# Query and key projections as pairs of 64-row products, maxima turned by VectorE, scores 12 groups behind

## The reference

```python
x = layernorm(x + attn(x, w_qkv, w_proj))            # 16 heads of 16, rotary turn of q and k
x = layernorm(x + xattn(x, ctx, Wq, bq, ..., Wo, bo)) # 16 heads of 16, keys and values from ctx
x = layernorm(x + ffn(x, ...))                        # two layers of local attention and MLP
```

## Time and profile before

| | us |
|---|---|
| median of 3 runs (2247.1 to 2249.8) | 2249.5 |
| span of the profiled execution | 2234.3 |
| TensorE busy in it | 2109.7 |
| VectorE busy | 1661.7 |
| ScalarE busy | 1501.9 |
| GpSimd busy | 1327.5 |
| 16-head part: first maximum to last `pv` | 43.0 to 983.2 |

### The profile page before, as it was taken

One profiled execution on the slowest core, in us unless ns is written; L12 is line 12 of the kernel. 1 busy time (PEld: TensorE's weight loads), 2 busy tenths in 40 slices (PEclk: granted clock), 3 DMA queues, 4 the chain that ended last, 5 costly groups with the idle time before them and its releaser, 6 DMA issues.

```text
span 2234.3 us, 44819 instructions
## 1 busy us (share of the span) xinstructions
PE 2109.7 (94%) x13992; PEld 1475.9 (66%) x13992; DVE 1661.7 (74%) x3987; ACT 1501.9 (67%) x3418; POOL 1327.5 (59%) x1376
## 2 busy tenths in 40 slices
PE   3899999999999999977999999899989999998998
PEld 2544444444444444346888888788878888887887
DVE  4777888777888888747888888656388888886675
ACT  2287777777888888855777777554367777775443
POOL 0344555533334444477888877454378887875775
PEclk7699999999999999999999999999999999999999
DMA  7667677665756666434545455300055554552111
GB/s 154 109 125 147 140 146 137 144 143 124 154 136 155 159 160 137 140 101 105 131 109 115 103 115 110 93 26 6 1 138 116 111 113 107 108 114 62 58 62 43
DMA packets 201337, 248.92 MB, mean 111 GB/s; under 512 B 26584, under 2 KB 119512, under 8 KB 201112
## 3 DMA queue, kind: packets, MB, share of 16 engines
q1 hardware_dynamic: 198552, 237.68, 47.7%
q0 software_dynamic: 2560, 8.39, 1.1%
HBM read 97.47 MB, written 63.44 MB: 72 GB/s over the span
## 4 chain that ended last, share of the span: by engine, by line
PE 77%; DMA 5%; POOL 5%; SPq 4%; ACT 3%; DVE 3%; issue 2%; POOLq 0%; ACTq 0%; DVEq 0%
PE PS L485 14%; PE PS L487 12%; PE PS L486 12%; PE PS L606 9%; PE PS L590 8%; PE PS L573 5%; PE PS L699 5%; PE PS L675 5%; PE PS L684 4%; DMA KS<-hs 3%; PE PS L659 2%; SPq L1496 2%; SPq L1464 1%; ACT PT L827 1%; DMA hs<-HL 1%
## 5 line engine op out<-in xcount | busy, mean ns | idle before, releaser
L1003 DVE TENSOR_REDUCE MX<-PS 128x1 f32<-128x512 f32 x1024 | 642.5, 682 | 167.1 <-PE PS L573 156.9
L827 ACT ACTIVATE PT<-PS 128x512 f32<-128x512 f32 x1024 | 546.2, 599 | 129.5 <-PE PS L590 127.6
L573 PE MATMUL PS<-KS,QS 48*128 48x512 f32 x1024 | 357.0, 454 | 43.7 <-DMA KS<-hs 33.5
L590 PE MATMUL PS<-QS,KS 50*128 50x512 f32 x1024 | 385.5, 456 | 6.4 <-ACT PT L827 6.0
L590 PEld LDWEIGHTS PS<-QS,KS 50*128 50x128 f32 x1024 | 164.9, 187 | 270.5 <-issue 212.3
L1369 POOL TENSOR_TENSOR PB<-PB,RC 128x512 f32<-128x512 f32 (+1 forms) x256 | 250.6, 999 | 48.6 <-DVE RC L1123 48.6
L606 PE MATMUL PS<-PT,VP 128*17 128x512 f32 x2048 | 273.6, 606 | 2.9 <-ACT OT L834 2.9
L890 ACT ACTIVATE PB<-PB,NMf 128x256 f32<-128x256 f32 (+1 forms) x512 | 242.6, 478 | 8.6 <-DVE NMf L1114 8.5
L573 PEld LDWEIGHTS PS<-KS,QS 48*128 48x128 f32 x1024 | 171.5, 192 | 108.0 <-issue 59.3
L1349 POOL TENSOR_TENSOR RI<-RI,mhalf 128x8 f32<-128x8 f32 x128 | 214.1, 1672 | 10.7
L1114 DVE CUSTOM_DVE_ANT_0 PB<-PS,mk 128x256 f32<-128x256 f32 (+1 forms) x512 | 175.7, 385 | 54.4 <-PE PS L675 54.2
(11 more groups left out here) (182 smaller groups left out, 5054.4 us busy)
## 6 DMA issues: line engine op xcount, KB each, us to landing
qT<-QN SPq DMA_DIRECT2D x384, 128.0 KB, 2.4
hs<-HL SPq DMA_DIRECT2D x64, 512.0 KB, 3.8
kT<-kT SPq DMA_DIRECT2D x256, 128.0 KB, 2.5
QS<-hs SPq DMA_DIRECT2D x192, 128.0 KB, 5.9
KS<-hs SPq DMA_DIRECT2D x192, 128.0 KB, 8.0
od<-OT SPq DMA_DIRECT2D x64, 256.0 KB, 5.9
OC<-od SPq DMA_DIRECT2D x32, 256.0 KB
cst<-rs SPq DMA_DIRECT2D x32, 256.0 KB
```

Source lines behind the costliest of these rows:

```text
L573: pe.matmul(PS[:, bank, :], QS[rows, s, h // 2, qt * P:(qt + 1) * P], KS[rows, s, h // 2, :], start=True, stop=True).then_inc(fills("amax" ...
L590: pe.matmul(PS[:, bank, :], KS[rows, s, pair, kt * P:(kt + 1) * P], QS[rows, s, pair, :], start=True, stop=True).then_inc(fills("score", v ...
L827: act.activation(PT[:, kt % 2, 2 * i + half], PS[:, TURNS["score", vb, g, kt, half, i][0], :], ACT.Exp).then_inc(drains("score", vb, g, kt ...
L1003: dve.tensor_reduce(MX[:, vb % 2, h // 8, qt, c:c + 1], PS[:, TURNS["amax", vb, h, qt][0], :], AX, ALU.max).then_inc(drains("amax", vb, h, ...
```

## The change

1. `rope` and `bias1` of all batches but batch 0: the six 128-row products of a tile become twelve products of 64 rows. `project_rows` does two tiles at once: in its first stage rows 0 to 63 add to tile 0 and rows 64 to 127 to tile 1, in its second stage the other way round. The second stage comes one pair of maxima and scores after the first, and waits until the first has ended. The two tiles hold two banks of the ring of four.
2. Self batches take xT from DRAM (`x_T`, a transposed copy of x among the inputs): a DMA of 512 KB (`load_xt`), `xt_hi` on ScalarE, `xt_lo` on GpSimd. The `tr` of self batches is gone. `load_x` stays, for the residual. At the start SyncE now issues x of batches 0, 1 and 2, `ident`, `bq` and `bb` after the first stacking, and after them `load_xt` of batch 1.
3. The maxima are turned by one VectorE transpose (32 x 32 blocks, 128 x 64 elements) for each half, and then go out to DRAM (`ms`) in two DMAs and back into QS in two more. `maxtr` and `negmax` are gone. Rows 48 and 49 of KS hold minus one.
4. Scores are 12 groups behind the maxima (`LAG`), so there are 268 groups.
5. The orders are written anew, in 96 places a step (three a slot), and every stage has a new place: `val` is a step earlier, for one. `LAST_STEP` keeps its distance from the end.

```diff
+LAG = 12
...
+    (0, "xt_hi", (1,), -1), (1, "norm", (1,), 4), (3, "ot_out", (0,), 1), (4, "mix", (0, 0), -1), (5, "max_out", (1,), 1), (5, "maxturn", (1,), 1),
+    (6, "ot", (0,), 1), (9, "out_hi", (1,), 3), (13, "rope", (0,), -1), (13, "max_in", (1,), 1), (15, "rope_out", (0, 0), -1),
+    (15, "mix", (0, 1), -1), (15, "rope_out", (0, 1), -1), (15, "sums", (), 2), (16, "mix_sum", (0, 0), -1), (19, "rope", (1,), -1),
...
+    (31, "collect", (0,), 2), (32, "mix", (1, 1), -1), (34, "heads_lo", (0, 0), -1), (35, "mix_sum", (1, 0), -1), (39, "heads_hi", (0, 1), -1),
+    (40, "mix_sum", (1, 1), -1), (43, "collect", (1,), 2), (45, "max_out", (0,), 0), (46, "heads_hi", (1, 0), -1), (47, "out_lo", (1,), 3),
+    (47, "maxrows", (0,), 0), (49, "heads_lo", (0, 1), -1), (49, "heads_lo", (1, 0), -1), (49, "heads_out", (0, 1), -1),
+    (50, "heads_out", (1, 0), -1), (50, "heads_lo", (1, 1), -1), (50, "scale", (0,), 2), (52, "heads_out", (1, 1), -1), (53, "ot", (2,), 1),
+    (53, "maxturn", (0,), 0), (54, "rstd", (0,), 3), (55, "proj", (0,), 3), (55, "heads_hi", (1, 1), -1), (56, "res", (0,), 3), (58, "rstd", (1,), 3),
+    (60, "max_in", (0,), 0), (65, "ot_out", (1,), 1), (65, "stats", (0,), 3), (71, "stack", (0,), -1), (73, "proj", (1,), 3), (74, "res", (1,), 3),
+    (75, "out_hi", (0,), 2), (76, "ot", (3,), 1), (77, "val_out", (0,), -1), (78, "stats", (1,), 3), (79, "val", (0,), -1), (79, "val_out", (1,), -1),
+    (79, "load_xt", (), -2), (80, "val", (1,), -1), (81, "ot_out", (2,), 1), (82, "norm", (0,), 3), (82, "scale", (1,), 2), (84, "out_lo", (0,), 2),
...
+    (1, "out_lo", (0,), 3), (1, "tr_hi", (0,), -1), (3, "tr", (0,), -1), (3, "inv_out", (), 2), (3, "tr_hi", (1,), -1), (4, "tr_lo", (0,), -1),
+    (4, "tr_lo", (1,), -1), (4, "tr", (1,), -1), (4, "maxturn", (1,), 1), (5, "out_lo", (1,), 3), (6, "ot", (0,), 1), (7, "bias1", (0,), -1),
+    (7, "ctx_lo", (0,), -1), (8, "load_ctx", (), -1), (8, "ctx_lo", (1,), -1), (9, "bias1_out", (0, 0), -1), (9, "bias1_out", (0, 1), -1),
+    (13, "max_out", (1,), 1), (17, "norm", (1,), 4), (22, "max_in", (1,), 1), (22, "ctx_hi", (0,), -1), (24, "ctx_hi", (1,), -1),
+    (25, "heads_lo", (0, 0), -1), (26, "add_bo", (), -1), (28, "stack", (1,), 0), (28, "ot_out", (0,), 1), (29, "collect", (0,), 2),
...
+    (30, "ot", (1,), 1), (32, "heads_lo", (0, 1), -1), (32, "max_out", (0,), 0), (33, "heads_hi", (0, 0), -1), (35, "heads_hi", (0, 1), -1),
...
+    (36, "heads_out", (0, 0), -1), (38, "bias1", (1,), -1), (39, "bias1_out", (1, 0), -1), (39, "bias1_out", (1, 1), -1), (41, "maxrows", (0,), 0),
+    (43, "heads_hi", (1, 0), -1), (47, "heads_out", (0, 1), -1), (49, "heads_lo", (1, 0), -1), (50, "heads_lo", (1, 1), -1), (52, "rstd", (0,), 3),
+    (53, "heads_out", (1, 0), -1), (54, "maxturn", (0,), 0), (54, "proj", (0,), 3), (54, "res", (0,), 3), (54, "ot", (2,), 1), (57, "spread", (), 2),
...
-    out += [("load_x", 2), ("load_bias",)]
...
+    out += [("load_x", 0), ("load_x", 1), ("load_x", 2), ("load_bias",)]
...
+                if kind in ("rope", "bias1"):
+                    put(step, place, (kind, vb) + part + (0,))
+                    seconds[96 * step + place + (1, 2, 1)[place % 3]] = (kind, vb) + part + (1,)
...
+    for n in range(16 * min(lags), 16 * NV + LAG + 1):
...
+            slot = 2 * n + half
             for i in range(2):
-                both = [("score", b, g, k, half, i), ("amax", a, 4 * g + 2 * i + 1 - half, k)]
+                a, b = n, n - LAG
+                both = [("score", b // 16, b // 4 % 4, b % 4, half, i), ("amax", a // 16, 4 * (a // 4 % 4) + 2 * i + 1 - half, a % 4)]
...
+                out += [seconds.pop(3 * slot + i)] if 3 * slot + i in seconds else []
+                out += places.pop(3 * slot + i, ())
+            if half and 0 <= n - LAG - 1 < 16 * NV:
+                p = n - LAG - 1
+                out.append(("pv", p // 16, p // 4 % 4, p % 4))
+            out += places.pop(3 * slot + 2, ())
...
-        elif kind in ("tr", "rope", "bias1", "val", "maxtr", "proj", "amax", "fold"):
+        elif kind in ("rope", "bias1") and a[0]:
+            for tile in range(2 - 2 * a[2]):
+                use((kind,) + a[:2] + (tile,), 4 + ring[0] % 4)
+                ring[0] += 1
+        elif kind in ("tr", "rope", "val", "proj", "amax", "fold"):
...
+            def project_rows(vb, qk, step, kind):
+                if step:
+                    pe.wait_ge(sem["row_halves"], 4 * (vb - 1) + 2 * qk + 2)
+                for kc in range(2):
+                    for n, (a, b) in enumerate(((0, 0), (0, 1), (1, 0))):
+                        for rows in range(2):
+                            tile = step ^ rows
+                            cols_ = slice(tile * P, (tile + 1) * P)
+                            m = pe.matmul(PS[:, TURNS[kind, vb, qk, tile][0], :], W[HALVES[rows], kc, a, qk, cols_], xT[HALVES[rows], kc, b],
+                                          start=step == kc == n == 0, stop=step == kc == 1 and n == 2)
+                            if kc == 1 and n == 2:
+                                m.then_inc(fills(kind, vb, qk, tile) if step else sem["row_halves"], 1)
+
             def weights_ready(kind, j):
                 pe.wait_ge(sem["w_lo"], n_weight(kind, j, 1))
 
             def rope(vb, qk, tile):
-                pe.wait_ge(*drained("tr", vb, 0))
-                pe.wait_ge(*drained("tr", vb, 1))
+                pe.wait_ge(sem["x_lo"], 2 * vb + 2)
                 weights_ready(0, qk)
-                bank = vacant(pe, "rope", vb, qk, tile)
-                project(vb, qk, tile, qk, bank).then_inc(fills("rope", vb, qk, tile), 1)
+                if vb == 0:
+                    bank = vacant(pe, "rope", vb, qk, tile)
+                    project(vb, qk, tile, qk, bank).then_inc(fills("rope", vb, qk, tile), 1)
+                    return
+                if tile == 0:
+                    for half in range(2):
+                        vacant(pe, "rope", vb, qk, half)
+                project_rows(vb, qk, tile, "rope")
...
-            def maxtr(vb, half):
-                pe.wait_ge(sem["max_parts"], 2 * (2 * vb + half + 1))
-                bank = vacant(pe, "maxtr", vb, half)
-                for qt in range(4):
-                    m = pe.transpose(PS[0:16, bank, qt * P:(qt + 1) * P], f(MB[:, half, qt]).rearrange("p a h -> p (a h)"), ident[:])
-                m.then_inc(fills("maxtr", vb, half), 1)
...
-                pe.wait_ge(sem["negmax_in"], 32 * (2 * vb + g // 2 + 1))
+                pe.wait_ge(sem["max_in"], 32 * (2 * vb + g // 2 + 1))
...
+            def xt_hi(vb, kc):
+                act.wait_ge(sem["xt_in"], 16 * (vb + 1))
+                act.copy(xT[:, kc, 0], xT0[:, kc, 1]).then_inc(sem["x_hi"], 1)
...
-            def negmax(vb, half):
-                act.wait_ge(*filled("maxtr", vb, half))
-                if vb or half:
-                    act.wait_ge(sem["negmax_in"], 32 * (2 * vb + half))
-                else:
-                    act.wait_ge(sem["ones_k"], 64)
-                act.activation(NM[:], PS[0:16, TURNS["maxtr", vb, half][0], :], ACT.Copy, scale=-1.0).then_inc(drains("maxtr", vb, half), 1)
...
+            def maxturn(vb, half):
+                dve.wait_ge(sem["max_parts"], 2 * (2 * vb + half + 1))
+                if vb:
+                    dve.wait_ge(sem["max_out"], 32 * (2 * vb + half - 1))
+                dve.transpose(MT[:, half].rearrange("p k c -> p (k c)"), f(MB[:, half]).rearrange("p k c -> p (k c)")).then_inc(sem["max_turned"], 1)
...
+            def xt_lo(vb, kc):
+                pool.wait_ge(sem["x_hi"], n_xhi(vb, kc))
+                pool.tensor_tensor(xT[:, kc, 1], xT0[:, kc, 1], f(xT[:, kc, 0]), ALU.subtract).then_inc(sem["x_lo"], 1)
...
+            def load_xt(vb):
+                if vb:
+                    sp.wait_ge(*filled("val", vb - 1, 1))
+                sp.dma_start(xT0[:, :, 1], t["x_T"][:, vb * S:(vb + 1) * S].rearrange("(k p) s -> p k s", p=P)).then_inc(sem["xt_in"], 16)
...
+                sp.dma_start(ident[:], t["c_ident"]).then_inc(sem["ident"], 16)
...
-            def negmax_out(vb, half):
-                sp.wait_ge(*drained("maxtr", vb, half))
+            def max_out(vb, half):
+                sp.wait_ge(sem["max_turned"], 2 * vb + half + 1)
+                if vb:
+                    sp.wait_ge(sem["max_in"], 32 * (2 * vb + half - 1))
+                for k in range(2):
+                    v = t["ms"][half, k].rearrange("x (b j) -> b x j", b=4)
+                    sp.dma_start(v, MT[:, half, k]).then_inc(sem["max_out"], 16)
+
+            def max_in(vb, half):
+                sp.wait_ge(sem["max_out"], 32 * (2 * vb + half + 1))
                 if vb >= 2:
                     sp.wait_ge(*filled("score", vb - 2, 2 * half + 1, 3, 1, 1))
                 for k in range(2):
-                    sp.dma_start(f(QS[48 + k:P:64, vb % 2, 4 * half:4 * half + 4]), f(NM[8 * k:8 * k + 8])).then_inc(sem["negmax_in"], 16)
```

(36 more changed lines are left out.)

161 lines of the change are left out of this document (68 added, 93 removed).

## The result

The changed kernel takes 2271.3 us (2265.0 to 2278.5, 4 runs) against 2248.3 (4 runs) for the kernel before, measured beside it: a ratio of 1.0114, 95% interval 1.0085 to 1.0143. Measured a second time, the ratio was 1.0089 (1.0050 to 1.0128). It is slower by about 1%, 23 us; 2225 was forecast. The span is 2263.1 us. The span of 2234.3 before was of a quick execution: in later profiles the executed time lies 1.8 us over the span (2242.9 against 2241.1), not 15.2, so that one stood some 12 us under its median.

What follows compares the result with a forecast made beforehand. The 16-head part was taken as a chain of TensorE's order. Terms -2 - 11 - 12 + 9 - 10 + 11 - 9 = -24 us gave 2225 us against the median 2249.5; own range 2210 to 2238.

Steps and rivals of the forecast that it cites:

- the way of the maxima: Each step's maxima through DRAM in two transfers: 9.8 to 13.2 us against 11.6 available; no wait in most steps.
- rival B: 4.1 us per landing makes every first score of a half 1.6 us late, 30 times, 48 us: 2273 us; chance 0.13.
- No transposes of x: Self batches 2 to 7: TensorE's transposes and a wait for xT go, 1.8 us a step, -11 us.
- the transposed x behind the stacking: Its DMA lands late, ScalarE then TensorE wait: 1 us in 6 self steps, 0.3 in 9 others, +9 us.
- Rival D: 512 KB more in the DMA queue of self steps, ScalarE waiting in each; 2240 to 2250 us, no change; chance 0.13.
- The start: Transposed x of batch 1 lands late, TensorE stands until 66, maxima of batch 1 begin at 109.7: +11 us.
- 64-row products: Projections of the 16-head part in row halves: two tiles 2.66 us, 2.41 without the wait; -0.15 a step, -2 us.
- Turning of maxima: TensorE no longer turns the maxima twice a step: 0.8 us a step, -12 us; VectorE's transpose taken as nothing.
- Four groups fewer: Last step, scores only: four fewer groups at 2.59 us each, -10 us.
- Old stalls: Two long steps lost 5 + 6 us with waits for GpSimd's maxima; 9 of 11 us go, -9 us.

Runs made afterwards that it cites:

- the kernel with the maxima mended: Changed kernel with the maxima turned by TensorE and moved SBUF to SBUF, and transposed x of batch 1 asked for early: 2222.7 us, ratio 0.9912 to the kernel before.
- The first experiment: Changed kernel with the maxima's read ahead of later heads transfers, and in cross steps their write at place 48: 2290.3 us, ratio 1.0212 to the kernel before.

## Why the prediction was wrong, step by step

**The step that failed is "the way of the maxima": "I take no wait in most steps".** The working had named all of it, even the three transfers of heads in front of the read, and had between 9.8 and 13.2 us for a cover of 11.6; then it took the end that gave nothing. The runs show, in the step at 563, 13.5 us for a cover of 11.2: 3.4 until the turn is done, 3.6 until the read is issued, and 6.5 from there to the score. By the forecast these were 2.8, 3.5 to 5.2 and again 3.5 to 5.2: it is the read, landing behind the heads, that lies outside. In five later cross steps the read is issued only 5.5 to 6.0 us after the write, with two issues of `cst`, 2.4 us, in between. The price is shown by the kernel with TensorE's turn: 20 to 26 us over all (31 with the start in time), where the forecast booked a gain of 12.

It is rival B's mechanism, but not its count: B had 1.6 us at each of 30 halves, 48 us, and the waits were 18, 40.5 us, of 0.2 to 5.4. That B's 2273 is so near to the measured 2271.3 is in part luck, since B had the transposed x at -2 and the runs show +13.

**"No transposes of x", -11, and "the transposed x behind the stacking", +9:** together -2, measured +13, for batches 2 to 7 and on the kernel with the maxima mended. The second had the right mechanism (ScalarE late, exponentials behind, then TensorE), and its 9 us are what ScalarE stood (8.9), though most of it in the first step and not 1 us in each. The first is the mis-sized one: 1.8 us a step were said and the group shows 1.2. That is 4 us of the 15 between -2 and +13. The rest may be the lower clock behind the waits, as in the first step, where a wait of 3.4 us goes with some 5 us lost; no run shows it. Rival D's sign, ScalarE waiting in each self step, came in three of them.

**The start, +11 (bounds 5 and 16):** measured 9 to 15 by itself and 20 with the maxima mended (0.9999 to 0.9912). Mechanism and place right, the wait for the low part forecast until about 66, seen until 64; the maxima of batch 1 forecast at 109.7, seen at 112.0. The constants' issues took 7.3 us where 0.8 was said.

**64-row products, -2:** two tiles 2.53 where 2.66 was said; 3 to 4 us against the kernel before. Right.

**Turning of maxima, -12:** 0.9 us a step by the steps of 53.5 and 54.4; 0.8 was said. Right as a cost of TensorE. VectorE's turn is 0.24 us, so "nothing" was right too; that it stands 2.6 us behind reductions was in the working.

**Four groups fewer, -10:** from the last maxima to the last `pv` it was 50.2 us and is 38.2. Right.

**Old stalls, -9:** the waits for GpSimd's maxima went, the new ones took their place.

The three stretches agree: the start and the end came about as forecast, and between them, where -25 was said, it is +21. Two transfers put in place of TensorE's work each cost more than they freed. The Trainium skill (DMA: Bandwidth & Descriptors, Anatomy of one DMA), from which the prediction quotes 2.0 us of fixed cost, gives it for transfers that GpSimd issues; these are SyncE's. Of the two landings of the last step the read's 2.12 us is near it, the write's 3.96 is not.

Without both, and with x of batch 1 early, what is left of the change is 1.5% faster than the kernel before (2208.7 us against 2243.1 beside it). From the 2249.5 of the forecast that would be 2217.

## What to carry to other kernels

Work taken off the busiest engine isn't a gain if a transfer with a due time takes its place: compare the engine's price (0.9 us a step here) with the lateness that the transfer has in the fullest stretch of the queue, with everything issued ahead of it. Here a sum that came out on both sides of its cover, 9.8 to 13.2 against 11.6, was a wait in seven of eight cross steps. In the orders of the queue that were tried the wait for the maxima shrank and other waits, for stacked heads and for VectorE, grew. And look where an in-order issuer stands: a place ahead of what it waits for (32 against 54) holds back everything behind it and then lets it go at once. The first experiment moved the place to 48, behind two of the heads, and other transfers were late instead.

## What was not expected of the hardware

In each cross step with such a wait of TensorE the mean granted clock was 0.89 to 0.97, where the step without one had 1.00: the step at 743 waited 4.2 us for QS and 3.1 for VectorE and was 9 us longer than the one at 452. The waits alone don't make up the difference; the seven steps are 1.5 to 5.1 us longer than 53.5 and their waits. The first score behind a wait can be seen at the lower clock, 0.76 us where one at full clock lasts 0.50:
```profile
663.12 0.76 PE L618 MATMUL PS<-QS,KS 50*128 50x512 f32 x1 [3.80 <-DMA QS<-ms]
```
A small read on GpSimd's queue, with nothing of its own in front, took 4.1 to 6.8 us to land beside the heads' transfers.
